# A routed two-layer FFN on one core: the W2 splits move behind the PSUM fills, and only into tiles whose next tile keeps its expert

## The reference

```python
w_bot = einsum('bg,got->bot', cond_8, weight * mask)
c = einsum('bnt,bot->bno', x, w_bot) + bias          # the conditioned rows
top1 = argmax(c @ gate_w.T + gate_b)                 # one expert per token
for e in range(8):
    h = relu(c @ w1[e].T + b1[e])
    y = h @ w2[e].T + b2[e]
    out += where(top1 == e, y, 0)
return x + out
```

## Time and profile before

| | us |
|---|---|
| median of 3 executions | 173.21 (172.95 to 176.34) |
| the profiled execution | 172.72 |
| its span, first to last instruction | 170.9 |

### The profile page before, as it was taken

How to read it: one execution, slowest core, us unless ns; L and a number is a source line. 1 busy time by engine, 2 the same in 40 slices (tenths; PEclk the granted TensorE clock), 3 DMA queues, 4 the chain that set the end, 5 groups by cost and what they waited for, 6 DMA issues and landing times.

```text
span 170.9 us, 6123 instructions
## 1 busy us (share of the span) xinstructions
PE 156.6 (92%) x1807; PEld 132.9 (78%) x1807; DVE 112.2 (66%) x217; ACT 106.7 (62%) x192; POOL 60.1 (35%) x59
## 2 busy tenths in 40 slices
PE   5999899994899999799799799999999999999970
PEld 2347588742689999799789799999999998898850
DVE  0396899980957768999999996345872552258300
ACT  3505988103295988999999968466754465566300
POOL 8300000037830255065666466442464201220222
PEclk9999999999999999999999999999999999999998
DMA  3999999949849788999999912322301101000100
GB/s 71 345 410 411 409 400 385 368 110 332 257 135 314 224 300 303 339 314 295 323 300 344 315 63 84 98 84 65 94 33 42 45 23 35 31 10 31 36 19 19
DMA packets 13797, 33.40 MB, mean 195 GB/s; under 512 B 2619, under 2 KB 6843, under 8 KB 13632
## 3 DMA queue, kind: packets, MB, share of 16 engines
q1 hardware_dynamic: 8288, 24.39, 40.8%
q0 software_dynamic: 2688, 6.30, 11.8%
q10 hardware_dynamic: 2784, 2.26, 4.0%
HBM read 30.06 MB, written 6.95 MB: 217 GB/s over the span
## 4 chain that ended last, share of the span: by engine, by line
PE 57%; DMA 18%; issue 9%; ACT 7%; ACTq 3%; DVE 1%; POOL 1%; SPq 1%; DVEq 1%; POOLq 0%
PE psum L944 21%; PE psum L928 19%; DMA wsp<-w_all 14%; PE psum L828 6%; PE psum L864 4%; PE psum L855 3%; DMA rows_in<-both_rows,tok_of_slot 2%; DMA both_rows<-stage 2%; ACT wsp L513 2%; ACT psum L543 2%; PE psum L916 1%; PE psum L841 1%; PE psum L812 1%; ACTq L284 1%; ACT stage L523 1%
## 5 line engine op out<-in xcount | busy, mean ns | idle before, releaser
L944 PE MATMUL psum<-wsp,hT 128*128 x504 | 58.5, 273 | 1.5 <-issue 1.1
L944 PEld LDWEIGHTS psum<-wsp,hT 128*128 128x128 f16 x504 | 48.1, 98 | 7.8 <-issue 2.6
L763 DVE SCALAR_TENSOR_TENSOR hT<-psum,hT 128x512 f16<-128x512 f32 x42 | 27.3, 687 | 22.6 <-ACT hT L560 22.2
L430 POOL DMA_INDIRECT out<-rows_in,tok_of_slot x17 | 19.9, 1170 | 58.7 <-DVE rows_in L768 58.7
L423 POOL DMA_INDIRECT rows_in<-both_rows,tok_of_slot x17 | 23.4, 1376 | 36.1 <-issue 36.1
L543 ACT ACTIVATE psum<-b_col 128x1024 f32 x21 | 21.5, 1022 | 21.3 <-issue 21.3
L928 PE MATMUL psum<-xs,w1s_own 128*128 128x128 f16 x528 | 31.6, 219 | 0.8 <-issue 0.8
L928 PEld LDWEIGHTS psum<-xs,w1s_own 128*128 128x128 f16 x528 | 30.1, 98 | 2.2 <-issue 1.8
L928 PE MATMUL psum<-xs,stage 128*128 128x128 f16 x480 | 28.4, 219 | 2.8 <-ACT psum L543 2.8
L928 PEld LDWEIGHTS psum<-xs,stage 128*128 128x128 f16 x480 | 27.3, 98 | 3.9 <-issue 2.2
L560 ACT ACTIVATE hT<-psum 128x512 f16<-128x512 f32 x42 | 22.9, 588 | 4.2 <-PE psum L928 2.4
(11 more groups left out here) (113 smaller groups left out, 138.9 us busy)
## 6 DMA issues: line engine op xcount, KB each, us to landing
wsp<-w_all SPq DMA_DIRECT2D x32, 512.0 KB
wsp<-cond_w SPq DMA_DIRECT2D x4, 512.0 KB, 6.8
wsp<-x_t SPq DMA_DIRECT2D x2, 1024.0 KB, 10.7
both_rows<-x_rows ACTq DMA_DIRECT2D x2, 1024.0 KB, 14.8
b_all<-b SPq DMA_DIRECT2D x1, 1024.0 KB, 18.2
both_rows<-stage SPq DMA_DIRECT2D x1, 768.0 KB, 7.3
both_rows<-stage SPq DMA_DIRECT2D x1, 512.0 KB, 6.1
both_rows<-stage SPq DMA_DIRECT2D x1, 384.0 KB, 4.9
```

Source lines behind the costliest of these rows:

```text
L430: g.indirect_dma_start(out, token(i), res(i % RING), None, bounds_check=TOK - 1, oob_is_err=False).then_inc(stored[i % RING], 16)
L763: v.scalar_tensor_tensor(hT[:, b, 1, q * HALF:(q + 1) * HALF], ps_h[b][q], 0.0, hT[:, b, 0, q * HALF:(q + 1) * HALF], ALU.max, ALU.subtrac ...
L944: last = t_.matmul(ps_y[b], hT[:, b, hp, c * P:(c + 1) * P], w, start=False, stop=(c == KH - 1 and w is low), skip_group_check=True)
```

## The change

Three things change. The goal becomes a count: `stays[j]` is 1 where tile position j has the same expert as the one before it, its running sum is compared with the expert number, the larger is multiplied by 2 and capped at 14. The splits of a tile move to the end of that tile's program on both engines. One `w1_low` of tile 0 moves behind the plan. With these inputs the new goals give these splits: tiles 0, 1, 2 and 3 two each; tiles 4 to 7 none; tile 8 two (the next tile's expert, 5, needs them); tile 9 none; tiles 10 and 11 two each; none after.

```diff
-        usual_goal = sb("usual_goal", [P, NT])
+        stays = sb("stays", [P, NT])
...
-            iota(usual_goal[:, :], [[3, NT // 2], [1, 2]], base=-3)
+            g.memset(stays[:, :], 0.0).then_inc(consts, 1)
...
             def tile(i, b, r, turn, plan):                       # ScalarE
                 if_used(act, used, i + 1, lambda: x_hi(i + 1, 1 - b))
                 if_used(act, used, i + 1, lambda: w1_high(i + 1, 1 - b, plan.next_expert, plan.next_expert - plan.expert))
-                if_used(act, used, i + 1, lambda: split_chunks(act, high_late, plan.goal, plan.next_goal))
                 next_plan = following_plan(act, i, plan)
                 if_used(act, used, i + 1, lambda: seed_h(i + 1, 1 - b, plan.next_expert))
                 if_used(act, used, i, lambda: h_hi(i, b))
                 if_used(act, used, i, lambda: seed_y(i, b, plan.expert))
+                if_used(act, used, i + 1, lambda: split_chunks(act, high_late, plan.goal, plan.next_goal))
...
-            w1_low(0, 0, 0, 0)
             dve.wait_ge(tok_ps, 1)
             v.tensor_scalar(tok_of_slot[:, :], ps_tok, float(TOK), None, ALU.add).then_inc(routed, 1)
...
-            then(v.tensor_scalar(goal_f[:, 0, :], tile_e[:, :], float(CPL), None, ALU.mult))
-            then(v.tensor_tensor(goal_f[:, 0, :], goal_f[:, 0, :], usual_goal[:, :], ALU.max))
-            then(v.tensor_scalar(goal_f[:, 1, :], goal_f[:, 0, :], float(W2_CHUNKS - EARLY), 0.0, ALU.min, ALU.max))
+            then(v.tensor_tensor(stays[:, 2:NT], tile_e[:, 2:NT], tile_e[:, 1:NT - 1], ALU.is_equal))
+            then(v.tensor_tensor_scan(goal_f[:, 0, :], ones[:, 0:NT], stays[:, :], 0.0, ALU.mult, ALU.add))
+            then(v.tensor_tensor(goal_f[:, 0, :], goal_f[:, 0, :], tile_e[:, :], ALU.max))
+            then(v.tensor_scalar(goal_f[:, 1, :], goal_f[:, 0, :], float(CPL), float(W2_CHUNKS - EARLY), ALU.mult, ALU.min))
...
             v.nop().then_inc(experts_known, 1)
+            w1_low(0, 0, 0, 0)
             w1_low(0, 0, 1, 0).then_inc(w1_ready, 1)
...
             def tile(i, b, r, turn, plan):                       # VectorE, behind y_out, x_lo and w1_new
-                if_used(dve, used, i + 1, lambda: split_chunks(dve, low_late, plan.goal, plan.next_goal))
                 next_plan = following_plan(dve, i, plan)
                 if_used(dve, used, i, lambda: h_lo(i, b, plan.goal))
+                if_used(dve, used, i + 1, lambda: split_chunks(dve, low_late, plan.goal, plan.next_goal))
```

## The result

The changed kernel takes 184.68 us (median of 6 executions, 183.34 to 185.28), the kernel before 173.1 beside it: 1.063 times as long, 95% interval 1.059 to 1.067. (Two of the six executions of the kernel before were slow ones, at 176.34 and 176.6; ratios are taken over fast executions alone, so they are not quite the quotients of the medians, here 1.067.) The forecast was 181.5 us within 178 to 185. The profiled execution took 184.58 us with a span of 182.8, the mean granted clock is 0.972.

A forecast was written before the change was run, and what follows sets the result against it. TensorE, 92% busy, was taken as the bound, with splits at the heels of the weight loads. 172.72 + 9.3 (waits, less savings) + 0.2 (tile 8) - 1.0 (loads) = 181.2; forecast 181.5 us, own range 179.5 to 183, with rivals 178.0 to 185.0.

The forecast's parts named there:

- the rivals: Alternatives to the forecast: clock falls (chance 0.20), loads gain more (0.17), faster (0.03), no effect (0.03).
- What bounds the kernel: Tile loop: TensorE, 92% busy, loses 3.4 us before tiles 5, 7 and 9; splits already run at the loads' heels.
- Term 1: Tiles 1 to 3: second splits wait for chunks 12, 16 and 20; layer 1 of tile 5 starts 11.7 us late.
- Term 2: Tiles 5 to 9 run at 5.51 us, saving 2.3 us; two splits in tile 8 cost 0.2.
- Term 3: Weight loads while tiles 1 to 5 stand: they gain 0 to 3.2 us, taken as 1.0.
- The clock: Rival: TensorE's clock falls in stands before tiles 3 and 5, adding 0 to 5.3 us, 2.7 taken; chance 0.20.
- The sum: Whole kernel: 172.72 + 9.3 + 0.2 - 1.0 = 181.2 us; forecast median 181.5 us, slower by 4.8%.
- Term 4: Before the loop: the moved `w1_low` brings 0, being hidden; without that cover a cost of 0.4 us at most.

The follow-up runs named there:

- e7: Kernel before with the splits at each tile's end and goals of one split per tile: 169.6 us, ratio 0.980.
- e3: Changed kernel with the goal's count begun at -1 instead of 0: 176.38 us, ratio 1.009.
- e6: Changed kernel with four weight chunks in flight instead of three: 178.96 us, ratio 1.037.
- After: The changed kernel itself, against the kernel before: 184.68 us, ratio 1.063.
- e4: Changed kernel with 42 extra matmuls in front of the transposes for tiles 4 and 6: 181.56 us, ratio 1.046.
- e5: Changed kernel run once more, unchanged, beside a later group of runs: 183.64 us, ratio 1.058.
- e2: Changed kernel with its new goals but the splits back at their old place: 182.16 us, ratio 1.049.
- e1: Kernel before with only the splits moved to each tile's end, old goals kept: 171.81 us, ratio 0.989.
- e8: Kernel before with goals of one split per tile, splits at their old place: 170.16 us, ratio 0.982.
- e9: Kernel before with only the one `w1_low` moved behind the plan: 174.81 us, ratio 1.004.

## Why the prediction was right, and where it was off

The way and the size were right, and so was the mechanism, the wait for chunks. But the result lies outside the forecast's own 179.5 to 183; it lies in 178 to 185 because that range was widened for the rivals, and near its upper end. Had the clock cost the whole of the 5.3 us that the prediction allowed it at most, the time would have been past 185.

**What bounds the kernel: right.** The 3.4 us in front of tiles 5, 7 and 9 were all there was to win in the loop. e7 takes them away and comes out 3 to 4 us under the kernel before. One reading was incomplete: ScalarE stood for a chunk before three splits, not two; the third, before the split at 60.91, was 0.84 us. It supports the same conclusion.

**Term 1, the waits that come: right, place and size.** The three layers 1 were forecast at 64.7, 72.5 and 82.5 and stood at 63.94, 71.42 and 82.35. That it is the landing of the last chunk asked for, and nothing else about the goals, was shown from two sides: e3 asks for chunk 16 instead of 20, e6 lands chunk 20 4.9 us sooner, and each time tile 5 moved along (74.02, 77.46). In five traces, After, e3, e4, e5 and e6, layer 1 of tile 5 follows the start of the split on that chunk by 5.89 to 5.97 us.

**Term 2, the waits that go: right.** Tiles 6 to 9 follow each other at 5.51 us, and the 2.35 us between tiles 5 and 9 came back. The 0.2 for tile 8 was 0.0.

**Term 3, the loads: the 1.0 us was not there, and one trace could not have shown it.** I reasoned that the late scatters and gathers would leave some of the DMA engines to the weights, and took 1.0 of a possible 3.2. Chunk 20 landed at 76.09 instead of 75.9. My own pair of windows had said so the earlier trace rows: 1.96 us a chunk with little beside it. What I read as a bound by bandwidth was a bound by what is in flight. e6 shows it: a fourth chunk in flight brings what freer engines did not. By the rule of the Trainium skill ("DMA: Bandwidth & Descriptors", Issuing engines are not separate DMA queues) transfers of all issuers interleave on the same engines; that fits a DMA share of 0.84 in After, where the three loads did not fill them and little was to be had from what others left. How far the loads gain from late tiles stays open, because the landing of chunk 20 varies by itself. The issue of chunk 23 behind it stands at 76.47, 78.08 and 75.57 in After, e5 and e4, at 74.40 in e2, and at 76.33, 76.99, 76.84, 78.66 and 77.07 in the kernels whose first tiles hardly stand (before, e1, e7, e8, e9). A gain of 1 us cannot be told from that scatter; the 4 us of e6 can.

**The clock: a rival that I held at 0.20 was the case.** This is the step that failed. The forecast's sum left the clock at full speed and priced its fall at 2.7 us, as the half of a possible 5.3. It fell twice; the first was hidden, the second cost 2.64 us, and e4 takes it away. (In e5 it cost 1.3.) The size of 2.7, half of a bound, was met by luck rather than worked out. I had argued that a slow layer 1 of tile 3 would shorten the second stand. It did not, since tile 4 waits for chunk 16 in any case and so starts at the same time, slow or fast (71.42 in After and in e4). The stand of 4.7 us stood in my own working; the earlier trace rows showed that some 3 us without matmuls were enough at the end of the program. The rule of the Trainium skill ("TensorE: Matmul & The Clock Gate", Part 1: The HAM clock gate), that the clock of an idle TensorE falls to half and returns only after sustained work, is what the windows show: 0.50 in 82.3 to 87.4, with TensorE busy all that time.

**The sum.** 181.2 + 1.0 (no gain of the loads) + 2.6 (clock) - 0.15 (tile 5) - 0.2 (tile 8) = 184.5, against 184.58 in the profiled execution. It is a balance of this one execution, drawn up afterwards; e5 comes to 184.70 with a later chunk and a cheaper clock.

**Term 4: nothing won,** as forecast. That the move might cost 0.4% was not foreseen and is not explained.

## What to carry to other kernels

Work done ahead of need is only free if its input is there: before moving a stage to an earlier slot, write the landing time of each transfer beside the slot that would ask for it, for an engine that works through its program in order passes the wait on to everything behind (here 2.91 us of ScalarE's waiting for chunk 20 became a stand of 5.26 of TensorE). Spread such work evenly, so that no slot is longer than the bound engine's pitch; here one split per tile instead of one and two in turn won 2% (0.980, interval 0.971 to 0.989), and 'only where there is room' lost 6%. When a stand of TensorE is forecast, price the slower clock behind it too (1.3 and 2.6 us here), and ask whether another wait hides it.

## What the runs showed of the hardware that was not expected

A fourth load of 512 KB in flight raised the rate from 271 to 337 GB/s in the same window, and the DMA share from 0.84 to 0.99, although a share of 0.84 had looked nearly full.

The clock can also fall behind a short stand. In front of the loop TensorE waits some 2.2 us for the gathered rows. In e7 the clock was at the lower level behind it, and layer 1 of tile 0 took 4.07 us instead of 2.84, hidden by what tile 1 waits for:

```profile
41.81 0.41 PE L916 MATMUL psum<-ident,rows_in 128*128 128x128 f32 x2 [2.25 <-DMA rows_in<-both_rows,tok_of_slot]
...
43.62 4.07 PE L928 MATMUL psum<-xs,w1s_own 128*128 128x128 f16 x48
```

The same fall stands in the traces of e2, e3, e5 and e6 (layer 1 of tile 0 at 3.57 to 4.23 us), behind stands of 2.15 to 2.27 us. In the kernel before, After, e1, e4 and e9 stands of 2.14 to 2.27 us in the same place left the clock at full speed. After and e5 are one kernel, once without the fall and once with it. So the length of a stand alone does not tell whether the clock falls, and what decides was not found.
